# A two-layer transformer kernel: stage one in another order, the routing spread over the slots, and attention's projection moved

## The reference

```
xn = layernorm(x)
x  = x + linear_attention(xn) + mx_linear(xn)     # layer 0
xn = layernorm(x)
x  = x + attention(xn) + moe(xn)                  # layer 1
```

```
p = softmax_over_b'( q[b] . k[b'] / sqrt(8) );  out[b] = sum_b' p * v[b'];  out @ out_w.T + out_b
```

## Time and profile before

| | us |
|---|---|
| median of 3 runs | 407.75 |
| lowest, highest | 403.55, 407.75 |
| the profiled execution, its own time | 408.82 |
| its span, first to last instruction | 405.9 |
| busy: PE | 325.6 |
| busy: DVE | 342.2 |
| busy: POOL | 236.5 |
| busy: ACT | 187.4 |
| start of the first slot of stage two | 187.5 |

### The profile page before, as it was taken

How to read it: one execution, slowest core, us unless ns; L and a number is a source line. 1 busy time by engine, 2 the same in 40 slices (tenths; PEclk the granted TensorE clock), 3 DMA queues, 4 the chain that set the end, 5 groups by cost and what they waited for, 6 DMA issues and landing times.

```text
span 405.9 us, 5042 instructions
## 1 busy us (share of the span) xinstructions
PE 325.6 (80%) x1455; PEld 238.8 (59%) x1455; DVE 342.2 (84%) x846; ACT 187.4 (46%) x502; POOL 236.5 (58%) x157
## 2 busy tenths in 40 slices
PE   0179889889889875706029999999999999999995
PEld 0047667868768675704016666666666666666662
DVE  4875889797876765599999899999999999999891
ACT  0553567876866735703022352625326262442521
POOL 9053584473563521094075959778695987867450
PEclk9996989999999988776759999999999999999999
DMA  7810000110110112120000000000010000000000
GB/s 184 263 23 1 2 0 2 53 52 2 52 53 1 53 52 97 66 52 1 0 1 0 2 1 26 2 26 0 1 28 0 26 2 27 0 2 26 0 26 27
DMA packets 13248, 12.49 MB, mean 31 GB/s; under 512 B 1549, under 2 KB 9925, under 8 KB 13221
## 3 DMA queue, kind: packets, MB, share of 16 engines
q1 hardware_dynamic: 10944, 10.10, 7.9%
q0 software_dynamic: 736, 0.95, 1.1%
q10 hardware_dynamic: 1540, 1.12, 1.0%
HBM read 5.88 MB, written 2.10 MB: 20 GB/s over the span
## 4 chain that ended last, share of the span: by engine, by line
PE 53%; DVE 25%; issue 7%; POOL 6%; ACT 5%; DMA 1%; ACTq 1%; POOLq 0%; DVEq 0%
PE Q L838 18%; PE VK L838 15%; PE T L838 9%; PE ND L838 7%; POOL prod_qk L778 3%; POOL prod_pv L788 2%; DVE rope_a L1248 2%; DVE rope_b L1250 2%; PE T L834 2%; PE Q L834 2%; DMA headmask<-in_c_headsel 1%; DVE attn L1280 1%; DVE chosen L1414 1%; DVE scr L1344 1%; DVE den L1277 1%
## 5 line engine op out<-in xcount | busy, mean ns | idle before, releaser
L788 POOL TENSOR_TENSOR prod_pv<-prob,qkv 128x1024 f32<-128x1024 f32 x32 | 69.6, 2212 | 45.0 <-DVE att L1361 24.2
L689 ACT ACTIVATE sg<-Q 128x512 f32<-128x512 f32 x72 | 43.1, 598 | 97.7 <-PE Q L838 94.9
L778 POOL TENSOR_TENSOR prod_qk<-qkv 128x1024 f32<-128x1024 f32 x32 | 75.9, 2397 | 16.7 <-DVE scr L1344 16.7
L838 PE MATMUL VK<-hid,w 128*128 128x512 f32 x144 | 74.5, 599 | 0.0
L838 PE MATMUL Q<-xT_hi,w_hi 128*128 128x512 f32 x72 | 52.3, 727 | 0.7 <-ACT combT L675 0.7
L1444 DVE TENSOR_TENSOR sgc<-ND,sg 128x512 f32<-128x512 f32 x64 | 43.7, 683 | 6.7 <-PE ND L838 4.6
L1457 DVE TENSOR_TENSOR hid<-T,sgc 128x512 f32<-128x512 f32 x64 | 43.6, 682 | 0.3
L838 PE MATMUL T<-xT_hi,w_hi 128*128 128x512 f32 x72 | 28.8, 401 | 17.1 <-DVE hid L1457 17.1
L838 PE MATMUL Q<-bias,ones 128*128 128x400 f32 (+1 forms) x64 | 29.7, 464 | 14.3 <-DVE xTs_lo L1299 9.2
L1344 DVE TENSOR_REDUCE scr<-prod_qk 128x128 f32<-128x1024 f32 x32 | 38.5, 1208 | 0.0
L1361 DVE TENSOR_REDUCE att<-prod_pv 128x128 f32<-128x1024 f32 x32 | 38.3, 1198 | 0.0
(11 more groups left out here) (189 smaller groups left out, 795.9 us busy)
## 6 DMA issues: line engine op xcount, KB each, us to landing
xT_hi<-xTs_hi SPq DMA_DIRECT2D x8, 256.0 KB, 2.3
xT_lo<-xTs_lo SPq DMA_DIRECT2D x8, 256.0 KB, 2.3
out_x<-fin SPq DMA_DIRECT2D x8, 256.0 KB, 2.3
x<-in_x SPq DMA_DIRECT2D x2, 256.0 KB, 4.8
wraw<-in_w1T SPq DMA_DIRECT2D x1, 512.0 KB, 9.7
w<-in_w2T SPq DMA_DIRECT2D x1, 512.0 KB, 6.0
wraw<-in_w3T ACTq DMA_DIRECT2D x1, 512.0 KB, 3.2
sel<-in_c_sel POOLq DMA_DIRECT2D x4, 128.0 KB, 2.8
```

Of the source, the lines that this page charges most:

```text
L689: act.activation(sg[:, side(half, s), :], QB[side(half, s)][:, :], ACT.Silu).then_inc(sg_ready, 1)
L778: pool.tensor_tensor(prod_qk[:, t % 2], bc(qkv2[:, TH * half + t, j, 0:D], 1, NB), qkv2[:, :, j, D:2 * D], ALU.mult).then_inc(qk_prod, 1)
L788: pool.tensor_tensor(prod_pv[:, t % 2].rearrange("p (h e) b -> p b h e", e=HD), bc(prob[:, t], 3, HD), qkv2[:, :, j, 2 * D:QKV].rearrange( ...
L838: return pe.matmul(o, lhsT, rhs, start=start, stop=stop)
```

## The change

- Slots take another order: n % 4 is the tile, n // 4 the half, so slots 0 to 3 need only batches 0 to 3 and the first half of the routing.
- `route` is cut into seven pieces. Those of half 0 stand in steps 9 to 11 of stage one on DVE, the last two behind the pipeline; those of half 1 stand in slots 0 to 3 (`route_later`). POOL's wait for `comb2_ready` 2 is gone. The second `combT` is made in slot 3.
- Slots 0, 1 and 2 get their own schedules on DVE (`first_slot`, `second_slot`, `third_slot`), later ones `later_slot`, in which `weighted` comes before the attention work of each slice. The exponential comes in slice 5, 4, 2 and then 1, and on ACT behind `yT`.
- `scr` and `prob` are laid out with the batch innermost (`[t, h, b]` in place of `[t, b, h]`).
- The projection of attention is no longer part of the sum in `VK`. `output_back` puts, for each of the four tiles, the transpose of `yT` and the product of `attT` with `wout2` into the same columns of `Q2`.
- Stage one: another order of each engine's step. `qfT` uses bank T0 in place of T1. The low parts of w1 and w3, the clearing of `sel` and its loads go to POOL in steps 9 and 10; the load of w3 goes to SP's queue.

```diff
         def slots(eng, slot):
             for n in range(NSLOT):
-                slot(n, n // 2, n % 2)
+                slot(n, n % NJ, n // NJ)
-        COMB_SLICE = 3
+        COMB_SLOT, COMB_SLICE = NJ - 1, 6
+        EXP_SLICE = [5, 4, 2] + [1] * (NSLOT - 3)
...
# sync
+                if b == NB - 3:
+                    sp.wait_ge(w1_ready, 1)
+                    sp.dma_start(wraw[:, 0:FW - P], d["w3T"]).then_inc(ld_w3, 16)
+                    sp.dma_start(wraw[:, FW - P:FW], d["w3sT"]).then_inc(ld_w3, 16)
...
# scalar, step
+                run(i, 1, xnT_evac)
                 norms_rooted(i)
+                if at(i, STEPS - 3):
+                    sigmoid(0)
                 weights_of_step(i)
-                run(i, 1, xnT_evac)
+                run_next(i, 5, l1_tile(2))
                 run(i, 2, xdT_evac)
-                run_next(i, 5, l1_tile(2))
                 act.wait_ge(rsqrt_step, RSQ * (i + 1))
                 run(i, 4, xn2_tiles(0))
+                run(i, 2, qfT_evac)
                 run(i, 4, xn2_tiles(1))
...
# scalar, slot
                     if s == 1:
-                        exp_done(n, half)
                         yT_evac(n)
+                    if (n, s) == (1, 2):
+                        evac(attT[:, :, :], tiles(Q2), (attT_ps, 1), [], attT_ready)
+                    if s == EXP_SLICE[n]:
+                        exp_done(n)
...
# gpsimd, step
+                if i == STEPS - 3:
+                    low_part(w1_lo[:, :], wraw[:, :], w1_hi[:, :], w1_hi_ready, w1_ready)
+                    sel_padded()
+                if i == STEPS - 2:
+                    low_part(w3_lo[:, :], wraw[:, :], w3_hi[:, :], w3_hi_ready, w3_ready)
...
-            pool.wait_ge(comb2_ready, 2)
...
+                if n < 2:
+                    normalise(n)
                 next_qk(3)
-                normalise(n)
+                if n >= 2:
+                    normalise(n)
...
# tensor, step (new order; the old one is printed above)
+                run(i, 1, xn_transposes)
+                run_next(i, 5, l1_tile(2))
+                run(i, 3, ffn_product)
+                run(i, 2, xd_transposes)
+                run(i, 2, qf_transposes)
+                run(i, 2, value_product)
+                run_next(i, 5, l1_tile(3))
+                run(i, 1, qkv_tile(0))
+                run(i, 2, numerators)
+                run(i, 1, qkv_tile(1))
+                run(i, 4, xn2_transposes(i))
+                run(i, 2, attn_transposes(i))
+                run(i, 1, qkv_tile(2))
+                run(i, 2, output_product)
+                run(i, 4, l1_tile(0))
+                run(i, 1, qkv_tile(3))
+                run(i, 4, l1_tile(1))
...
# tensor, slots
-            def attention_projection(n):
-                pe.wait_ge(attT_ready, n + 1)
-                mm(VK[:, :], wout2[:, :], attT[:, :, :].rearrange("p t f -> p (t f)"), False, False)
+                for t in range(TH):
+                    pe.matmul(Q2[:, t * P:(t + 1) * P], yT[:, t, :], ident[:, :], is_transpose=True, start=True,
+                              stop=False)
+                    m = mm(Q2[:, t * P:(t + 1) * P], attT[:, t, :], wout2[:, :], False, True)
+                m.then_inc(yback_ps, 1)
...
# vector, step (new order)
+                run(i, 1, mx_maxima)
+                rsqrt(i)
...
+                if at(i, STEPS - 1):
+                    route_top(0)
+                    route_chosen(0)
+                run(i, 2, features)
+                run(i, 3, projection_scaled)
...
+                run(i, 2, head_blocks)
+                run(i, 3, plus_ffn)
+                if at(i, STEPS - 3):
+                    route_pairs(0)
+                if at(i, STEPS - 2):
+                    route_allowed(0)
+                run(i, 1, mx_scales)
...
+                run(i, 1, rope_tile(0))
+                run(i, -1, stats(0, stats1_ready))
+                run(i, 2, attention)
+                if at(i, STEPS - 3):
+                    route_ranks(0)
+                run(i, 1, rope_tile(1))
+                run(i, 1, mx_magic)
+                run(i, 3, stats(1, stats2_ready))
+                run(i, 4, xn2T_lo_part)
+                run(i, 1, rope_tile(2))
+                if before_last(i):
+                    ln_values(i)
+                run(i, 1, rope_tile(3))
+                if before_last(i):
+                    rms_values(i)
...
# vector, slots
-            route(0)
-            scores(0, 0, 0)
-            scores(0, 1, 0)
-            route(1)
-            scores(0, 2, 0)
-            scores(0, 3, 0)
+            route_weights(0)
+            route_parts(0)
...
+            def route_later(n, s):
+                if (n, s) == (0, 7):
+                    route_pairs(1)
+                if (n, s) == (0, 8):
+                    route_ranks(1)
+                if (n, s) == (1, 1):
+                    route_allowed(1)
+                if (n, s) == (1, 8):
+                    route_top(1)
+                if (n, s) == (2, 0):
+                    route_chosen(1)
+                if (n, s) == (2, 5):
+                    route_weights(1)
+                if (n, s) == (3, 1):
+                    route_parts(1)
...
+            def first_slot(s):
+                if s < TH:
+                    scores(0, s)
+                if s == 4:
+                    less_max(0)
+                if s == 5:
+                    scores(1, 0)
+                    sum_of_p(0)
+                if s == 6:
+                    over_sum(0)
+                    dve.wait_ge(xT_kept, 32 * NB)
+                    values(0, 0)
+                if s == 7:
+                    scores(1, 1)
+                    values(0, 1)
+                if s == 8:
+                    values(0, 2)
+            def second_slot(s):
+                if s == 0:
+                    values(0, 3)
+                if s in (1, 2):
+                    scores(1, 1 + s)
+                if s == 3:
+                    less_max(1)
+                if s == 4:
+                    residual(0)
+                    scores(2, 0)
+                    sum_of_p(1)
+                if s == 5:
+                    over_sum(1)
+                if s >= 5:
+                    values(1, s - 5)
+                if s == 7:
+                    scores(2, 1)
+            def third_slot(s):
+                if s in (0, 1):
+                    scores(2, 2 + s)
+                if s == 1:
+                    less_max(2)
+                if s in (2, 3):
+                    scores(3, s - 2)
+                if s == 3:
+                    sum_of_p(2)
+                if s == 4:
+                    residual(1)
+                    over_sum(2)
+                if 4 <= s < 4 + TH:
+                    values(2, s - 4)
+                if s in (7, 8):
+                    scores(3, s - 5)
...
+            def later_slot(n, s):
+                more = follow(n) is not None
+                if s == 0:
+                    less_max(n)
+                if s == 2:
+                    sum_of_p(n)
+                if s in (1, 2, 7, 8) and more:
+                    scores(n + 1, {1: 0, 2: 1, 7: 2, 8: 3}[s])
+                if s == 3:
+                    over_sum(n)
+                if 3 <= s < 3 + TH:
+                    values(n, s - 3)
+                if s == 4:
+                    residual(n - 1)
```

317 lines of the change are left out of this document (147 added, 170 removed).

## The result

The changed kernel takes 411.41 us (median of four runs, 410.58 to 414.06) against 407.75 before (403.55 to 408.03). The ratio on record is 1.0138, interval 1.0085 to 1.0191; the quotient of the two medians is 1.009. It is slower by about 1%; the forecast was 401, with a range of 390 to 411. Its profiled execution took 411.27 us, with a span of 409.5 (405.9 before).

What follows compares the result with a forecast made beforehand. Work order set stage one and PE bounded stage two; after the change DVE would bound slots 0 to 3. Terms -7.4 - 3 + 1.5 + 1.6 + 0.4 = -6.9 gave span 399.0, forecast 401 us, range 390 to 411.

Steps and rivals of the forecast that it cites:

- slots 0 to 3: DVE bounds these slots: 107.0 us of work against PE's 96.4, plus 12 of waits for POOL; gain 7.4 us.
- slots 4 to 7: PE bounds these slots again; the new orders cost 1.6 us and the projection 0.4 in all.
- with no idle of DVE: Expected sign in slots 0 to 3: each takes 28 to 33 us on DVE, which never idles.
- the 4 of ACT at the start: Before DVE weights the first slice, ACT needs two table loads and three activations, 4 us in round numbers.
- DVE needs 22.7 + 2 where the slot is 24.1: Slots 4 to 7: DVE waits about 2 us before slice 2, adding 0.55 in three slots, 1.6 us.
- the forecast of -3: Stage one: the new order shortens a step from 15.91 to 15.43 us, -3 over seven full steps.
- In the drain I had +1.5: End of stage one: moved low parts, memset and routing groups cost 1.5 us, bounds -1 to +4.
- The layout gives: New layout of `scr` and `prob`: maximum and sum save 0.36 us each, 2.9 in four slots.
- The projection costs nothing: Projection moved out of the experts' sum on PE: 0 to 0.1 us a slot net, 0.4 in four slots.
- rival 3: POOL's product with `prob` slows from 2.21 to 3.3 us in the slots, +13, total 414; chance 0.08.
- rival 4: Stage one: `ln_values` or `rms_values` waits for POOL each step, 15.91 becomes 17, total 412; chance 0.10.
- Rival 2: Slots 0 to 3: POOL waits of 3.5 us a group, 18 in all, take the gain; 404 to 410; chance 0.27.
- Rival 1: Routing hides nearly whole, waits 4 instead of 12, stage one gives 1 us a step; 389 to 396; chance 0.15.

Runs made afterwards that it cites:

- e4: Changed kernel without the second half's routing (left out, so another output): 397.92 us, ratio 0.9843 to the kernel before.
- e9: Changed kernel, second half's routing whole ahead of the slots with slot 0's four scores among it, old orders in the slots: 398.42 us, ratio 0.9824.
- e5: e2 with two routing groups moved to where POOL stands and slot 2 normalised before the next slot's fourth product: 404.60 us, ratio 0.9982.
- e7: Changed kernel with POOL's attention products made for one batch or feature only (another output): 399.93 us, ratio 0.9882.
- e1: Changed kernel with ACT's exponential ahead of `yT` again in slots 3 to 7: 413.29 us, ratio 1.0202.
- e3: Changed kernel with DVE's score and sum ahead of the weighting of slice 2 again in slots 3 to 7: 407.36 us, ratio 1.0024.
- e6: Changed kernel with POOL's memset of `sel` moved from step 9 of stage one to behind the last reciprocal root: 412.44 us, ratio 1.0194.
- e2: Changed kernel with both ACT's and DVE's old orders restored in slots 3 to 7: 411.71 us, ratio 1.0146.
- e8: Changed kernel with the second half's routing not spread but whole ahead of the slots: 410.99 us, ratio 1.0157.

## Why the prediction was wrong

The profiled span can be laid beside the sum of the prediction term by term:

| | predicted | measured | miss |
|---|---|---|---|
| start of the slots | 172.3 - 3 + 1.5 = 170.8 | 174.8 | +4.0 |
| slots 0 to 3 | 4 + 107 + 12 = 123.0 | 301.2 - 174.8 = 126.4 | +3.4 |
| slots 4 to 7 | 94.5 + 2.0 = 96.5 | 401.5 - 301.2 = 100.3 | +3.8 |
| behind the last `hid` | 8.7 | 8.0 | -0.7 |
| span | 399.0 | 409.5 | +10.5 |

No single term carries the miss; three of a like size do, all to the same side. The forecast was a gain of 6.9 us.

**Slots 0 to 3: the step that failed is "with no idle of DVE".** DVE was busy 28.17 + 29.09 + 33.48 + 24.23 = 115.0 us in them, where I had 107 + 12 = 119. The waits for POOL in `route(1)` were 7.6 us and not 12: the third addition 2.19 for 0.27, `allowed` 2.37 for 0.20, `wsel` and `wsum` 1.9 and 1.6 more; two groups met a pause. What I had left out is idle time: 11.4 us, of which I had counted the 4 of ACT at the start. The waits of the trace give 5.9 for ACT's silu, 5.1 of it at the start, and 5.7 for PE's `ND`. The two large ones of these 5.7 come before PE's stand of 4.37 at 268.1 and have nothing to do with it: 2.91 at 240.3, behind PE's 3.84 for `att`, and 1.56 at 257.4, behind a stand of PE of 2.67 for `hid` at 250.6. I had put at nothing what the late exponentials of slots 0 to 2 do to the chain behind them (`values`, POOL's normalisation, PE's transposes), and e4 shows it without any routing. In e9, with the old orders, PE has no such stand and slots 2 and 3 take 24.0 and 24.2. DVE also has more to do in slot 2, which holds six scores: 26.45 us in e4 against 22.9 in e9. How much each edit of the orders is worth was not separated; e5 says that `normalise` ahead of the fourth product for slot 2 and the moved group are worth 1.6.

**Slots 4 to 7: the wait was seen and its price was not.** DVE stood 2.09 us before slice 2 (I had about 2) and its own work was 23.05 (I had 22.7). What I missed is a second wait, at the first weighting of the slot, where DVE now stands for PE:

```profile
327.72 0.69 DVE L1481 TENSOR_TENSOR sgc<-ND,sg 128x512 f32<-128x512 f32 x1 [0.64 <-PE ND L844]
```

23.05 + 2.09 + 0.64 = 25.8, the slot. (Its work is 0.35 above my 22.7; the subtraction of the maximum alone takes 1.50 us in slots 5 and 6, where it took 1.12.) The step that failed is "DVE needs 22.7 + 2 where the slot is 24.1": it took PE's line as full, while PE stood for DVE too (busy 24.8 of 25.8) and passed the delay on. e7 leaves POOL 0.4 us of it; e1 to e3 show that either order restored gives back 1.0 to 1.6 us of 1.8.

**Stage one.** The steady step is 15.6 us, before 15.9; I had 15.4. Four steps of 15.6 or 15.1 gave 1.6 us, but the step ahead of them takes 16.4 in nearly every execution of the new order, where the old one shows 14.7, and that takes it back: the forecast of -3 came to -1.1 at the reciprocal root of step 9 (138.7 against 139.8) and to nothing in the middle of the executions of the new order (138.7 to 141.4). In the drain I had +1.5, and it was +3.6; steps 9 and 10 take 17.7 + 8.8 us against 16.1 + 7.0, and the slots start 2.5 later than the last L1 tile ended before. I had costed the moved instructions one by one and not the fact that DVE got some 10 us of routing groups in three steps, and that its pauses there are partly waits for ACT, which no work of its own shortens (e6).

**What held.** The layout gives 0.36 us on the maximum and as much on the sum. The projection costs nothing (24.0 in e2 against 24.1). `prod_pv` did not lengthen, so rival 3 is false, and POOL did not lengthen a steady step by standing in the way of root instructions, so rival 4 is false. Rival 2 saw that nothing would be gained, but by waits of 18 us for POOL, and they were 7.6; it stopped at 409, and its mechanism is false too. Rival 1, with waits of 4 and a faster stage one, is false for the changed kernel. The 13.3 us between the changed kernel and e4 are what `route(1)` costs in the slots. Its bare work is 11.6 by my estimate, and DVE has 0.65 us to spare in a slot. The prediction had the sum (107.0 us of DVE against 96.4 of PE) and did not draw from it that these four slots can hide 4 x 0.65 = 2.6 us of 11.6. So it never weighed the change against itself with `route(1)` ahead of the slots, which e8 finds level and e9, with the old orders, 13 us faster.

## What to carry to other kernels

Before work is spread beside a loop, multiply the slack of its engine by the number of turns: 4 x 0.65 us cannot hide 11.6, and what does not fit is paid in full (here 13.3 us). When an early iteration of a loop gets a schedule of its own, follow each chain that starts later in it to the engine that waits at its end: here an exponential moved by a few slices ended in 3.84 us of PE. The first half's routing, the same instructions, gained 5 us in the drain of a pipeline, where its engine had pauses of several microseconds. And when two fixes each bring a group of instructions to another place (e1, e2), look at what the shift now collides with before calling the theory false: e5 had the same cure and a different place for one group, and was 7 us faster.

## What the runs showed of the hardware

**POOL holds up DVE for whole instructions, and not only those with two inputs.** A copy of 128 x 256 from SBUF to SBUF with a single input took 2.12 us beside a product of POOL and 0.29 without; a `tensor_scalar` of eight numbers stood 4.95 us behind POOL's subtraction and its memset, which reads nothing. The match-replaces of the routing and the scores' reductions beside POOL's products, and sixteen of the routing's maxima beside its normalisation at 235.4, never stretched. Single lines of the changed kernel (least, middle and greatest ns):

```profile
L1439 DVE MAX8 top<-masked x32: 151/158/171, 166.2 to 236.3; 128x8 f32<-128x16 f32 x32
...
L1447 DVE MATCH_REPLACE8 chosen<-top,masked x32: 158/164/172, 167.8 to 244.2; 128x16 f32<-128x16 f32 x32
...
L1360 DVE TENSOR_REDUCE scr<-prod_qk x32: 1203/1207/1215, 179.4 to 376.9; 128x128 f32<-128x1024 f32 x32
```

The Trainium skill ("SBUF — State Buffer", section "SBUF: two separate sides") has an exclusive lock that is held for the whole instruction, by DVE instructions in a 2-port mode too; the copy and the memset agree with it. No row shows the mode in which DVE ran an instruction, so this is agreement and not proof.

**A stall of PE can be paid twice.** After the 3.84 us for `att` PE's matmuls came every 0.43 instead of 0.23 us. From the transposes of `att` to the `ND` matmul that DVE waits for took 3.04 us (236.51 to 239.55); the same matmuls at the end of slot 2, at the upper level of the clock, took 1.83 (273.68 to 275.51). So of DVE's 2.91 us about 1.2 is the clock, by my estimate from these rows. It is paid only where DVE then waits for PE: after the stall of 4.37 us the clock fell too, and DVE's waits up to the start of slot 3 are 0.44. The granted clock of that slot is 0.87; in slot 3 it is 0.89 in e2 and 1.00 in the changed kernel. How much of a slot's excess is clock and how much is waiting was not separated beyond this.
